# A state-space layer with routed experts on one core: semaphores set back inside the pass instead of behind it

## The reference

```
x = x + layernorm(ssm(layernorm(x)))
x = x + layernorm(experts(layernorm(x)))

ssm:     q = rope(x @ W_in[:256].T);  h = rmsnorm(q)
         z, xBC, dt = split(h @ W_zxbcdt.T);  dt = softplus(dt + dt_bias)
         xBC = silu(causal_conv4(xBC));  x, B, C = split(xBC)
         y = chunked_scan(x, dt, -exp(A_log), B, C) + D * x
         return rmsnorm(y * silu(z)) @ W_out.T + q
experts: shared: (silu(x @ sg.T) * (x @ su.T)) @ sd.T
         routed: 16 experts of 64, the best 2 of 4 groups, the best 4 in them,
         sum of weight * (silu(x @ g) * (x @ u)) @ d
```

## Time and profile before

| | |
|---|---|
| median of 3 runs | 3087.72 us |
| profiled execution | 3097.12 us |
| its span, first to last instruction | 3095.5 us |
| granted TensorE clock, mean share | 0.992 |
| busy: PE, PEld | 3013.1 us (97%), 2563.6 us (83%) |
| busy: DVE, ACT, POOL | 2401.3 us (78%), 1911.0 us (62%), 2052.0 us (66%) |
| DMA, mean over the span | 73 GB/s |

### The profile page before, as it was taken

One profiled execution on the slowest core, in us unless ns is written; L12 is line 12 of the kernel. 1 busy time (PEld: TensorE's weight loads), 2 busy tenths in 40 slices (PEclk: granted clock), 3 DMA queues, 4 the chain that ended last, 5 costly groups with the idle time before them and its releaser, 6 DMA issues. The chain is left out here.

```text
span 3095.5 us, 65583 instructions
## 1 busy us (share of the span) xinstructions
PE 3013.1 (97%) x21248; PEld 2563.6 (83%) x21248; DVE 2401.3 (78%) x5232; ACT 1911.0 (62%) x4117; POOL 2052.0 (66%) x2311
## 2 busy tenths in 40 slices
PE   5799999999999999999999999999999999999997
PEld 4688888888888888888888888888888888888876
DVE  5877887778887778887778887778787778877763
ACT  5566665666666566666556666566666666666562
POOL 2477666677666677666677666776666776666774
PEclk8999999999999999999999999999999999999998
DMA  3122222222222222222222222222222232222222
GB/s 127 42 70 90 75 79 64 68 68 89 75 67 69 71 74 82 79 68 62 65 88 79 79 69 61 68 89 78 80 62 68 68 89 75 77 67 68 68 77 48
DMA packets 153546, 227.35 MB, mean 73 GB/s; under 512 B 30624, under 2 KB 98976, under 8 KB 153504
## 3 DMA queue, kind: packets, MB, share of 16 engines
q1 hardware_dynamic: 136608, 210.05, 21.2%
q0 software_dynamic: 16896, 16.78, 3.5%
HBM read 174.87 MB, written 35.13 MB: 68 GB/s over the span
## 5 line engine op out<-in xcount | busy, mean ns | idle before, releaser
L659 POOL TENSOR_TENSOR hidL<-hid,hidH 128x512 fp32r<-128x512 f32 x384 | 559.5, 1457 | 166.8 <-ACT hidH L914 159.0
L914 ACT CAST hidH<-hid 128x512 fp32r<-128x512 f32 x384 | 236.9, 617 | 430.4 <-POOL hid L654 366.5
L1130 DVE SCALAR_TENSOR_TENSOR xc<-apb,cw,xc 128x511 f32<-128x511 f32 (+2 forms) x576 | 428.1, 748 | 77.3 <-ACT xc L834 49.2
L1626 PE MATMUL acc<-WDH,hidH 128*128 128x256 f32 x1536 | 456.3, 297 | 7.4 <-POOLq L661 4.4
L1626 PE MATMUL acc<-WDH,hidL 128*128 128x256 f32 x1536 | 429.5, 280 | 0.0
L1626 PE MATMUL acc<-WDL,hidH 128*128 128x256 f32 x1536 | 429.3, 279 | 0.0
L654 POOL TENSOR_TENSOR hid<-hid,cb 128x512 f32<-128x512 f32 x256 | 346.9, 1355 | 40.1 <-POOL zs L630 13.1
L1253 DVE TENSOR_TENSOR hid<-hid,fpb 128x512 f32<-128x512 f32 x384 | 259.9, 677 | 98.8 <-PE fpb L1448 87.7
L1448 PE MATMUL fpb<-fTh,UH 128*128 128x512 f32 x768 | 336.5, 438 | 0.0
L1448 PE MATMUL fpb<-fTh,GH 128*128 128x512 f32 x768 | 317.3, 413 | 0.4 <-DVEq L1041 0.4
L852 ACT ACTIVATE seg<-seg,acs 128x128 f32<-128x128 f32 x1024 | 313.4, 389 | 3.8 <-POOL seg L614 3.3
(11 more groups left out here) (191 smaller groups left out, 8624.0 us busy)
## 6 DMA issues: line engine op xcount, KB each, us to landing
seg<-acs_row SPq DMA_DIRECT2D x128, 512.0 KB, 4.4
cb<-c_row SPq DMA_DIRECT2D x512, 128.0 KB, 2.9
xsP<-in_x SPq DMA_DIRECT2D x32, 512.0 KB, 3.6
xc<-qrot SPq DMA_DIRECT2D x32, 512.0 KB, 3.3
xc<-in_x SPq DMA_DIRECT2D x32, 512.0 KB, 4.3
out<-xc SPq DMA_DIRECT2D x32, 512.0 KB, 2.9
out<-xn POOLq DMA_DIRECT2D x32, 512.0 KB, 6.3
ZL_loaded<-in_wzx_t SPq DMA_DIRECT2D x2, 512.0 KB, 4.6
```

The source lines that it names most:

```text
L659: own.do(G.tensor_tensor(hidL[:, j % 2, :], hid[:, j % 2, :], hidH[:, j % 2, :].bitcast(fp32), ALU.subtract))
L914: A.copy(hidH[:, j % 2, :], hid[:, j % 2, :]).then_inc(sem["hidden_high"], 1)
L1130: ins = V.scalar_tensor_tensor(xc[:, b, s:], src[:, 0:T - s], cw[:, b, TAPS - 1 - s:TAPS - s], xc[:, b, s:], ALU.mult, ALU.add)
L1626: ins = nc.tensor.matmul(dst, l[:, w, tk], r[:, j, :], start=j == 0 and t % 2 == 0 and n == 0, stop=j == HB - 1 and n == 2, skip_group_che ...
```

## The change

On VectorE, ScalarE and GpSimd a helper `settled(*names)` writes back the named semaphores at once and remembers them in `closed`; `settle` leaves out what is in `closed`. In the three lists of `iteration` such calls are put behind the last wait on each semaphore: 20 writes on VectorE, 13 on ScalarE, 14 on GpSimd. At the end of the pass 3, 6 and 5 remain. SyncE, PE and the parts outside `iteration` keep their order, and every computing instruction, wait and DMA stands in the same order on every engine as before.

```diff
@@ -384,9 +384,9 @@
                 if waiter == who and first:
                     eng.sem_inc(sem[n], k * int(first))
 
-        def settle(eng, who, part):
+        def settle(eng, who, part, closed=()):
             for n, (waiter, p_, k, _) in SEM.items():
-                if waiter == who and p_ == part and k:
+                if waiter == who and p_ == part and k and n not in closed:
                     eng.sem_inc(sem[n], -k)
 
         def now(name, n=1):
@@ -686,17 +686,26 @@
                 G.inc_swdge_sem([s_stored], [16], mode="sub")
                 pool.sem_inc(sem["xn_free"], 1)
 
+            closed = set()
+
+            def settled(*names):
+
+                for n in names:
+                    assert SEM[n][0] == "POOL" and n not in closed
+                    pool.sem_inc(sem[n], -SEM[n][2])
+                    closed.add(n)
+
             def settle_p():
-                settle(pool, "POOL", "p")
+                settle(pool, "POOL", "p", closed)
 
...
 
             def lead():
                 norm_px(); rope_sum(0); root_q(0); rope_sum(1); root_q(1)
@@ -716,13 +725,17 @@
                 if g: add_result(i - 2)
                 rest(1); rest(2); mask(0); hold_shift(); mask(1)
                 if g: result_stored()
-                decayed(0); decayed(1); rest(3); combine(4); gated(0); combine(5); rest(4); mask(2); decayed(2)
-                rest(5); norm_px(); mask(3); gated(1); combine(6); gated(2); rest(6); root_y(0); combine(7)
-                rope_sum(0); rest(7); norm_mixed(0); combine(8); gated(3); rest(8); root_q(0); combine(9)
-                root_y(1); rope_sum(1); rest(9); root_q(1); norm_mixed(1); norm_x1(0); combine(10); norm_x1(1)
-                combine(11); rest(10); rest(11)
+                settled("seg_loaded0", "seg_loaded1"); decayed(0); decayed(1); rest(3); combine(4); gated(0)
+                combine(5); rest(4); mask(2); settled("seg_loaded2"); decayed(2); rest(5); settled("xdt_ready")
+                norm_px(); settled("px_moments"); mask(3); gated(1); settled("seg_loaded3"); combine(6); gated(2)
+                rest(6); root_y(0); combine(7); rope_sum(0); rest(7); norm_mixed(0); combine(8); gated(3); rest(8)
+                settled("y_ready"); root_q(0); combine(9); root_y(1); settled("ssy_ready"); rope_sum(1); rest(9)
+                settled("rope_ready"); root_q(1); norm_mixed(1); norm_x1(0); combine(10)
+                settled("ssq_ready", "mixed_moments", "cb_loaded0"); norm_x1(1); settled("x1_moments"); combine(11)
+                rest(10); settled("product_ready"); rest(11)
                 settle_p(); settle_a(); settle_f()
                 if g: settle_g()
+                closed.clear()
                 own.settle()
 
             def tail(i):
...
@@ -966,19 +988,22 @@
                 begin("steady")
                 conv_first(4); silu_z(0, 0); silu_z(1, 0); f_high(0); f_high(1); conv_first(5); conv_silu(4)
                 silu_z(2, 0); conv_silu(5); exp_table(); softplus(); conv_first(0); silu_table(); silu_z(3, 0)
-                gate(0); conv_first(1); conv_silu(0); score_tanh(); conv_first(2); round_hidden(0)
-                conv_silu(1); gate(1); silu_z(0, 1); conv_silu(2); gate(2)
+                gate(0); settled("na_ready"); conv_first(1); settled("dt_read", "tmp_free"); conv_silu(0)
+                score_tanh(); conv_first(2); round_hidden(0); settled("logits_ready"); conv_silu(1); gate(1)
+                silu_z(0, 1); conv_silu(2); gate(2)
                 if g: final_norm()
                 conv_first(3); round_hidden(1); silu_z(1, 1); round_hidden(2); evac_B(); conv_silu(3); gate(3)
-                gate(4); evac_CB(); silu_z(2, 1); exp_table(); decays(); exp_seg(0); round_hidden(3)
-                exp_seg(1); silu_table(); gate(5); silu_z(3, 1); round_hidden(4); round_hidden(5); gate(6)
-                exp_table(); exp_seg(2); evac_y(0); norm_x(0); exp_seg(3); silu_table(); gate(7); square_y(0)
-                evac_xT(0); evac_y(1); round_hidden(6); square_y(1); round_hidden(7); gate(8); norm_x(1)
-                square_q(0); evac_y(2); evac_xT(1); square_y(2); round_hidden(8); gate(9); evac_y(3)
-                square_y(3); round_hidden(9); square_q(1); gate(10); h_high(0); h_high(1); gate(11); norm_x1(0)
-                round_hidden(10); norm_x1(1); round_hidden(11)
+                settled("conv_ready"); gate(4); evac_CB(); silu_z(2, 1); exp_table(); decays(); exp_seg(0)
+                round_hidden(3); exp_seg(1); silu_table(); gate(5); settled("acs_ready", "shared_ready"); silu_z(3, 1)
+                round_hidden(4); round_hidden(5); gate(6); exp_table(); exp_seg(2); evac_y(0); norm_x(0); exp_seg(3)
+                silu_table(); gate(7); square_y(0); settled("xn_free", "masked"); evac_xT(0); evac_y(1)
+                round_hidden(6); square_y(1); round_hidden(7); gate(8); norm_x(1); square_q(0); settled("px_norm")
+                evac_y(2); evac_xT(1); square_y(2); round_hidden(8); gate(9); evac_y(3); square_y(3)
+                settled("a_for_ACT"); round_hidden(9); square_q(1); settled("qrot_ready"); gate(10); h_high(0)
+                h_high(1); gate(11); settled("p_for_ACT"); norm_x1(0); round_hidden(10); norm_x1(1); round_hidden(11)
                 settle_p(); settle_a(); settle_f()
                 if g: settle_g()
+                closed.clear()
                 own.settle()
                 way.check(freed, "ACT")
 
...
@@ -1354,18 +1388,22 @@
 
             def iteration(g=True):
                 begin("steady")
-                dt_bias_add(0); dt_bias_add(1); conv(4); f_low(0); dt_bias_add(2); f_low(1); conv(5)
-                route_logits(); dt_bias_add(3)
+                dt_bias_add(0); dt_bias_add(1); conv(4); f_low(0); dt_bias_add(2); f_low(1); settled("fh_ready")
+                conv(5); route_logits(); dt_bias_add(3)
                 if g: final_moments()
-                dt_finish(); conv(0); up(0); conv(1); conv(2); route_scores(); evac_acs(); up(1)
-                route_groups(); up(2); conv(3); route_experts(); up(3); times_dt(0); times_dt(1); decay_CB(0)
-                up(4); new_state(0); chunk_y(0); up(5); state_part(1); decay_CB(1); new_state(1); times_dt(2)
-                chunk_y(1); moments_px(); up(6); state_part(2); decay_CB(2); y_low(0); new_state(2); chunk_y(2)
-                times_dt(3); decay_CB(3); x_low(0); y_low(1); up(7); rope(0); mixed_out(0); state_part(3)
-                up(8); chunk_y(3); y_low(2); x_low(1); add_x(0); up(9); y_low(3); rope(1); norm_q(0)
-                mixed_out(1); up(10); norm_q(1); h_low(0); add_x(1); h_low(1); up(11)
+                dt_finish(); conv(0); up(0); conv(1); conv(2); route_scores(); evac_acs(); up(1); route_groups()
+                up(2); conv(3); route_experts(); up(3); times_dt(0); times_dt(1); decay_CB(0); up(4)
+                settled("logits_made"); new_state(0); settled("ln_ready", "tanh_ready", "conv_first", "decay_ready")
+                chunk_y(0); up(5); state_part(1); decay_CB(1); new_state(1); times_dt(2); chunk_y(1); moments_px()
+                up(6); state_part(2); decay_CB(2); y_low(0); new_state(2); settled("xp_loaded"); chunk_y(2)
+                times_dt(3); decay_CB(3); settled("xdt_free", "exp_ready"); x_low(0); y_low(1); up(7); rope(0)
+                mixed_out(0); state_part(3); settled("q_kept"); up(8); chunk_y(3); y_low(2); settled("a_for_DVE")
+                x_low(1); add_x(0); settled("xh_ready", "x_loaded"); up(9); y_low(3); settled("yh_ready"); rope(1)
+                norm_q(0); settled("p_for_DVE"); mixed_out(1); settled("out_ready", "ry_ready"); up(10); norm_q(1)
+                h_low(0); add_x(1); settled("rq_ready", "mixed_stats"); h_low(1); settled("hh_ready"); up(11)
                 settle_p(); settle_a(); settle_f()
                 if g: settle_g()
+                closed.clear()
                 own.settle()
                 way.check(freed, "DVE")
 
```

More of the change, by code:

```diff
@@ L687, in result_stored @@
                 pool.sem_inc(sem["xn_free"], 1)
+            closed = set()
[4 more added lines that the diff above has]
+                    closed.add(n)
             def settle_p():
[L690 removed]
+                settle(pool, "POOL", "p", closed)
             def settle_a():
[L693 removed]
+                settle(pool, "POOL", "a", closed)
             def settle_f():
[L696 removed]
+                settle(pool, "POOL", "f", closed)
             def settle_g():
[L699 removed]
+                settle(pool, "POOL", "g", closed)
             def lead():
@@ L923, in final_norm, with settled @@
                 act.sem_inc(sem["normalised"], 1)
+            closed = set()
+            def settled(*names):
+                for n in names:
+                    assert SEM[n][0] == "ACT" and n not in closed
+                    act.sem_inc(sem[n], -SEM[n][2])
+                    closed.add(n)
             def settle_p():
-                settle(act, "ACT", "p")
+                settle(act, "ACT", "p", closed)
```

(6 more changed lines are left out.)

17 lines of the change are left out of this document (10 added, 7 removed).

## The result

The changed kernel took 3094.39 us (median of 11 runs, 3092.87 to 3097.03), the kernel before beside it 3087.49 (11 runs, 3085.80 to 3088.75): ratio 1.0024, interval 1.0015 to 1.0033. That is 6.9 us slower, where 3.0 us faster was forecast. The profiled executions say the opposite: 3097.12 us for the kernel before, 3094.05 for the changed one, 3.07 us less. Both are measured, and most of this study is about how they go together.

A forecast was written before the change was run, and what follows sets the result against it. PE, working in 97% of the span, was taken as the bound, so only its waits count. -4.8 us at project_z(2,0) plus 1.8 us of GpSimd lateness gave -3.0 us, hence 3084.7 us from 3087.72; range 3073 to 3093.

The forecast's parts named there:

- the last of the sum: Whole kernel: the 3.0 us saving, summed on the profiled execution, taken off the runs' median 3087.72 to give 3084.7.
- the 1.8 us for rest(10): GpSimd's end of pass: exposed writes leave rest(10) 0.06 us later a pass, 30 x 0.06 = 1.8 us lost.
- 0.30 us of room for late writes: GpSimd's L589 of norm_x1(0), 0.49 against 0.19: its 0.30 us would swallow the 0.18 to 0.27 of lateness left.
- The 0.16 at project_z(2,0): PE's wait for the bank that silu_z(0,0) empties would vanish: 0.16 us a pass, 4.8 us over 30 starts.
- the 0.9 us lead at conv_first(5): ScalarE's conv_first(4) comes 0.9 us earlier, but the lead ends at conv_first(5), which waits for PE's project_x(5).
- D: Rival, faster: part of the 0.9 us lead survives and shortens PE's L862 and L839 holds; 3060.7, half 3074; chance 0.18.
- an exposed write: GpSimd write not hidden under a running instruction: 0.09 us each, four such a pass, 0.36 us.
- the hold before down(10): PE's wait for GpSimd's rest(10) before loading down(10): would grow from 0.31 to under 0.45 us.
- gated(2)'s L629: GpSimd instruction drawn out to 2.31 us against 1.29: 1.0 us of room for xdt_ready and seg_loaded3 (0.18).
- VectorE at zero: VectorE's 20 moved writes cost PE nothing; three exposed ones, together 0.3 us, were taken as covered by waits.
- B: Rival, nothing comes through: GpSimd's lateness at down(10) reaches 0.16 us and eats the gain; 3087.7, chance 0.15.
- C: Rival, slower: a small GpSimd instruction at norm_x1(0) falls behind the second L1219, losing 0.4 us a pass; 3094.9, chance 0.12.

The follow-up runs named there:

- before_two: Kernel before with only GpSimd's writes y_ready (behind rest(8)) and rope_ready (behind rest(9)) moved: 3100.09 us beside 3087.14, ratio 1.0044.
- act_early: Kernel before with ScalarE's 13 writes moved and GpSimd 0.18 us earlier (two marks issued under root_q(1)'s first instruction): 3094.00 us beside 3098.02, ratio 0.9985.
- before_early: Kernel before with GpSimd 0.18 us earlier, two marks behind rest(9) issued under root_q(1)'s first instruction: 3096.89 us beside 3098.02, ratio 0.9997.
- dve_only: Kernel before with only VectorE's 20 writes moved, ScalarE's and GpSimd's left at the loop's end: 3097.17 us beside 3087.14, ratio 1.0036.
- before_again: Kernel before, unedited, run and profiled once more: 3097.60 us beside 3097.35, ratio 1.0002; profiled execution 3084.11 us.
- after_trim: Changed kernel with four GpSimd and two VectorE writes back at the loop's end and GpSimd 0.18 us earlier: 3093.53 us beside 3098.02, ratio 0.9985.

## Why the prediction was wrong

**The step that failed** is the last of the sum: "The median of the runs shown is 9.4 us lower, 3087.72; the same 3.0 off it gives 3084.7." The 9.4 us were set down as an offset of the profile, and a sum worked out in the held mode was carried to runs that were not in it. The two modes are 0.42 us a pass apart, 0.31 of it standing on the load of down(10), and 13.0 us in all. In the held mode L589 waits anyway, and lateness of GpSimd is largely hidden there; in the good one the same lateness makes it wait in the first place. So the term that was mis-sized is the 1.8 us for rest(10): 0.06 a pass was forecast, 0.09 measured in the held mode, and 0.47 where two writes of 0.08 us end the good mode (93.58 against 93.11, before_two; 13 us). The row was there: L589 at 0.49 was read as 0.30 us of room for late writes; it was also 0.3 us that a run without it would not pay. A profile 9.4 us above runs that agree within 1.4 us should have been asked which wait the runs do without. That 30 times 0.31 is 9.3 proves nothing, as the modes that were traced lie 13.0 apart: what the runs at 3087 have over 3084 stays open.

The gain was sized in the held mode too. In the good one project_z(2,0) is held less:

```profile
1053.02 0.27 PE L1626 MATMUL acc<-WDH,hidL 128*128 128x256 f32 x1
1053.13 0.37 PE L1448 MATMUL apb<-ZH,hTh 128*128 128x264 f32 x1
1053.34 0.28 PE L1448 MATMUL apb<-ZL,hTh 128*128 128x264 f32 x1
```

Steps of 0.11 and 0.21 make 0.08 us in place of 0.16 (0.08 to 0.11 over the passes of this trace), and ScalarE's part gives 0.11 a pass there (act_early against before_early): 2.4 to 3.3 us over 30 passes, not 4.8.

**What held, in the profiled mode.** The 0.16 at project_z(2,0), the death of the 0.9 us lead at conv_first(5) (the waits for L839 and L862 are unchanged, so D is out), 0.08 for an exposed write against 0.09, ScalarE's 0.20 and VectorE's 0.98, and the hold before down(10), 0.40 against "under 0.45". Their sum, 3094.1 for the profiled execution, came out at 3094.05, which is partly luck. The lateness left at rest(10) was 0.09, not 0.06, so that a held pass is only 0.06 shorter; the two passes without a hold gave back 1 us more; and two later profiles of the changed kernel took 3096.31 and 3095.30. Inside that sum two things were not as told: gated(2)'s L629 gave back 0.03 (2.31 to 2.28), not the 0.08 to 0.18 of the writes ahead of it, and L589 gave back 0.14 (0.49 to 0.35), not 0.18 to 0.27.

**VectorE at zero** was wrong. The pair behind add_x(0) was called covered because "rope(1) and mixed_out(1)" wait for PE. rope(1) and norm_q(0) do not: they follow up(9) and y_low(3) with no wait for PE between, and were 0.13 later. VectorE's part alone closes the good mode (dve_only); that these two writes of it would do so by themselves is argued from rows, not shown.

**B** (nothing comes through) did not happen in either mode. **C** gave the time, 3094.9, and the place, but not the point from which it decides: "a lateness of some 0.3 us". Writes of 0.16 us did it (before_two), and in the kernel before 0.03 us separate a caught L589 from a free one. It was priced as something that the writes would add, a small instruction behind the second L1219; in the changed kernel L589 still ends with the first of the two, as in the first profile, and the writes took away the mode in which it does not wait at all. That C's time is so near the 3094.39 is therefore partly luck.

The Trainium skill ("SBUF — State Buffer", Who interferes with whom) has VectorE's two-input instruction contend with a GpSimd instruction that reads SBUF, calls the shared ports an exclusive lock, and lets the order of issue decide who waits. The rows agree in the main: a caught L589 ends 0.05 us behind the end of the first L1219, whenever it started; but one that starts 0.01 us behind went free in before_again and was caught in after_trim. The same section says that tensor_scalar can take the shared ports as well, in the modes that use two ports and if its operands meet their conditions. norm_q, beside which powers were drawn out to 0.77 and 0.85, may be that case; no run here shows which mode it ran in.

**Open.** What chooses the mode at the start of a run, and why one chip mostly held the kernel before and another mostly did not, no run here shows. Nor does the edge of each instruction follow from these rows: GpSimd made 0.18 earlier was caught at another, and 0.01 us behind add_x(1) can be free or caught. Nor was the level between the two modes, where the kernel before ran at 3087 and at 3090, ever traced.

## What to carry to other kernels

When the profiled execution lies several us off runs that agree among themselves, find out which repeated wait makes the difference before anything is added to or taken off either; take a second profile if one can be had, and hold it against the runs as well: here the second one lay 13 us below them. On an engine that runs back to back into the wait that PE ends on, the price of an edit of 0.1 us is set less by its length than by which neighbour it falls behind. Writes that only need to happen once a pass belong where an engine is idle anyway: of the three parts only ScalarE's brought anything (0.11 to 0.16 us a pass in the traces), while taking apart VectorE's run at the loop's end cost 10 us by closing the good mode, and GpSimd's 8 us where the kernel was held already.

## What was not expected of the hardware

One program kept one of two schedules through a whole run, 0.42 us a pass apart (93.11 and 93.53), at the same granted clock (0.991 and 0.992). GpSimd's L589 on 128x2 elements takes 0.19 us, or 0.35 to 0.51 where it is caught behind VectorE's L1219, until 0.05 us behind that one's end; a power on as many takes 0.70, or 0.75 to 1.00. VectorE in turn takes 2.29 us for the two L1219 of add_x(0), during which GpSimd's L629 and L630 of gated(3) run, and 0.87 for those of add_x(1).
